# An adaLN transformer block on one core: output sent in two parts with an accumulating transfer, a new setup, a shorter calibration, explicit table loads, and the last pair split

## What is computed

```python
mod = (silu(c) @ wmod).reshape(B, 6, 1, -1)                 # B = 16 sequences, D = 256
sa, ca, ga, sb, cb, gb = mod[:, 0], ..., mod[:, 5]          # ga, gb: magnitude at least 0.25
h = layernorm(x) * (1 + ca) + sa                            # x: (16, 512, 256), float32
x = x + ga * attn(h)                                        # causal softmax of |q.k|/16, then Wo
h = layernorm(x) * (1 + cb) + sb
x = x + gb * ffn(h)
# ffn: cluster score -> calibrate (sigmoid, 8 knots, piecewise linear) -> argmax over 8 clusters
#      tile score of the chosen cluster -> calibrate -> argmax over 8 tiles -> gather 1 of 64 tiles
#      comp = tanh(gelu(h W1 + b1) W2 + b2); mag = relu(comp . w1 + b1') . w2' + b2'
#      y = layernorm(h + mag * direction * scale) * gamma + beta
```

## Time and profile before

| | us |
|---|---|
| three runs of the kernel | 470.21, 470.64 (median), 472.34 |
| the profiled execution | 471.67 |
| its span, first to last instruction | 469.8 |
| its mean granted TensorE clock | 0.931 of 2.4 GHz |

### The profile page before, as it was taken

The page is one execution under the profiler, slowest core; times in us unless marked ns, Lnnn a source line. Parts: engine busy times, 40 slices in busy tenths (PEclk is TensorE's granted clock), DMA queues, the critical chain, the costliest instruction groups (busy, mean ns, idle before and its releaser), DMA issues.

```text
span 469.8 us, 7656 instructions
## 1 busy us (share of the span) xinstructions
PE 399.8 (85%) x2072; PEld 308.7 (66%) x2072; DVE 398.5 (85%) x1367; ACT 296.5 (63%) x645; POOL 67.4 (14%) x82
## 2 busy tenths in 40 slices
PE   2697899999999999899989998999899999463330
PEld 2555578777777877687768776877677778452220
DVE  4417637387859899999999999999999899999996
ACT  2230365877698769676967697769776976651400
POOL 1002310302020002400250015001400220031040
PEclk9977899999999999999999999999999999796565
DMA  8503102101200213112310231122100210040112
GB/s 292 142 30 105 74 23 79 35 1 45 69 23 1 69 45 114 45 28 86 114 45 25 91 112 47 22 91 86 50 1 1 73 64 1 4 130 0 35 57 89
DMA packets 26234, 28.72 MB, mean 61 GB/s; under 512 B 3888, under 2 KB 21552, under 8 KB 26192
## 3 DMA queue, kind: packets, MB, share of 16 engines
q1 hardware_dynamic: 24160, 26.38, 17.8%
q10 hardware_dynamic: 2032, 1.85, 1.2%
HBM read 19.77 MB, written 8.45 MB: 60 GB/s over the span
## 4 chain that ended last, share of the span: by engine, by line
DVE 45%; PE 42%; issue 8%; ACTq 2%; ACT 2%; DVEq 0%
PE bank L511 8%; PE bank L530 8%; PE bank L490 6%; PE bank L500 6%; PE bank L553 3%; DVE y L1278 3%; DVE y L1246 3%; DVE x L1091 3%; DVE res L1288 3%; DVE st L1254 2%; DVE probs L1077 2%; DVE st L1046 2%; PE bank L520 2%; ACTq L680 2%; DVE v L1070 2%
## 5 line engine op out<-in xcount | busy, mean ns | idle before, releaser
L511 PE MATMUL bank<-h,g 128*128 128x128 f32 (+3 forms) x256 | 80.2, 444 | 4.9 <-DVE v L1070 4.9
L978 POOL TENSOR_TENSOR res<-x,gb_row 128x512 f32<-128x512 f32 x32 | 44.5, 1407 | 268.3 <-DMA out<-res 268.3
L530 PE MATMUL bank<-v,probsT 128*128 128x257 f32 x320 | 79.1, 382 | 0.0
L500 PE MATMUL bank<-m_ga,h 128*128 128x258 f32 x256 | 68.8, 394 | 5.2 <-DVE rows L1360 3.2
L530 PEld LDWEIGHTS bank<-v,probsT 128*128 128x128 f32 x320 | 57.1, 190 | 6.6 <-DVE y L1246 0.3
L490 PE MATMUL bank<-h,a_sb 128*128 128x512 f32 x128 | 60.4, 595 | 0.0
L511 PEld LDWEIGHTS bank<-h,g 128*128 128x128 f32 x256 | 44.7, 195 | 22.1 <-issue 8.5
L500 PEld LDWEIGHTS bank<-m_ga,h 128*128 128x128 f32 x256 | 47.7, 197 | 15.7 <-issue 4.3
L736 ACT ACTIVATE bank<-bank,v 128x128 f32<-128x128 f32 (+1 forms) x64 | 31.7, 495 | 41.4 <-PE bank L511 29.1
L1077 DVE CUSTOM_DVE_ANT_0 probs<-bank,cmask 128x128 f32<-128x128 f32 (+1 forms) x64 | 31.1, 485 | 23.3 <-ACT bank L736 23.3
L742 ACT ACTIVATE probs<-probs,negmax 128x128 f32<-128x128 f32 (+1 forms) x64 | 35.5, 557 | 5.9 <-DVE negmax L1077 5.9
(11 more groups left out here) (167 smaller groups left out, 770.1 us busy)
## 6 DMA issues: line engine op xcount, KB each, us to landing
x<-in_L_attn_x SPq DMA_DIRECT2D x16, 512.0 KB, 3.5
out<-res SPq DMA_DIRECT2D x16, 512.0 KB, 3.0
a_row<-gate_rows SPq DMA_DIRECT2D x16, 256.0 KB, 3.2
gb_row<-gate_rows SPq DMA_DIRECT2D x16, 256.0 KB, 3.2
wide<-in_L_wmod ACTq DMA_DIRECT2D x2, 768.0 KB, 7.6
res<-in_L_attn_Wq SPq DMA_DIRECT2D x1, 256.0 KB, 5.0
res<-in_L_attn_Wk SPq DMA_DIRECT2D x1, 256.0 KB, 7.3
res<-in_L_attn_Wo SPq DMA_DIRECT2D x1, 256.0 KB, 10.1
```

What stands on the lines that cost most here:

```text
L500: last = mm(ps[:, 0:VW], h[s][:, c, t * P:(t + 1) * P], m_ga[p % 2][s][:, c, :], start=(c == 0), stop=(c == KC - 1))
L511: last = mm(ps[:, 0:w], g[s][:, c, t * P:(t + 1) * P], h[s][:, c, 0:w], start=(c == 0), stop=(c == KC - 1))
L530: last = mm(ps[:, 0:D + 1], probsT[s][t][:, j * P:(j + 1) * P], v_sb[s][:, j, 0:D + 1], start=(j == 0), stop=(j == t))
L978: gp.tensor_tensor(res[:, 2 * u:2 * u + 2, :], x2[p % 2][s][:, t, :], gb_row[p % 2][s][:, 1:2, :].broadcast_to([P, 2, D]), ALU.add).then_i ...
```

## The change

Seven edits go together.

1. **The output is sent in two parts.** x2 is sent to `out` by SP as soon as it is there (`xo`). `ob` adds the gated beta row instead of `res`, so `res` holds the gated FFN alone, and POOL issues a transfer of it that adds into `out` (`ay`). `base` remains for the last two groups only, which are sent whole.
2. **calibrate** has ten instructions in place of twelve: the line of each of the seven segments is evaluated, masked and summed.
3. **Tables.** After `gelu` and after `tanh` the set that holds ln and exp is loaded by name.
4. **The last pair is two groups** of four tiles (groups 7 and 8) in the FFN; groups 0 to 6 are pairs.
5. **Setup.** silu is taken on the turned c; the gate row of sequences 0 and 1 is made directly on 128 partitions (`su_gax`, `sd_gax`), without the way through memory; biases are loaded by POOL; copies move from DVE to ACT; two of the first `a_xh` and one `a_h` are done by DVE; the signature and table constants are made by POOL (`sp_sig`, `sp_rest`) after the first `ms`.
6. **Orders**: every engine has a written order for the first steps, a loop for k = 5 to 7, and a written order for the end.
7. **The bank table** is new.

```diff
+            def xo(g, i):
+                p, s = of_group(g, i)
+                spq.wait_ge(x2_rdy, NT * (before(g) + i + 1))
+                spq.dma_start(out_v[GROUPS[g][i]], x2[p % 2][s][:, :, :]).then_inc(x2_sent[p % 2][s], 16)
...
+            def ay(g, i):
+                pool.wait_ge(alone_rdy, NT * (before(g) + i + 1))
+                pool.wait_ge(x2_sent[g % 2][i], 16 * (g // 2 + 1))
+                gp.dma_start(out_v[GROUPS[g][i]], res[:, NT * i:NT * (i + 1), :], accum_op=ALU.add).then_inc(summed[i], 16)
...
             def ob(g, t):
+                if g < BY_SUM:
+                    if t % NT == 0:
+                        need(dve, summed[t // NT], 16 * g)
+                    rest = gb_row[g % 2][t // NT][:, 1, :]
+                else:
+                    dve.wait_ge(base_rdy, 2 * (before(g) - before(BY_SUM)) + t // 2 + 1)
+                    rest = res[:, t, :]
-                stt(out=res[:, t, :], in0=y[:, t, :], scalar=ln3["rstd"][:, t:t + 1], in1=res[:, t, :],
-                    op0=ALU.mult, op1=ALU.add).then_inc(res_rdy, 1)
+                stt(out=res[:, t, :], in0=y[:, t, :], scalar=ln3["rstd"][:, t:t + 1], in1=rest,
+                    op0=ALU.mult, op1=ALU.add).then_inc(alone_rdy, 1)
...
             def base(g, u):
+                pool.wait_ge(summed[0], 16 * BY_SUM)
+                need(pool, sent, 16 * (g - BY_SUM))
...
+                if i == 3:
+                    m(ts(low, pos, 0.5, ROUND - 0.5, ALU.max, ALU.add))
+                elif i == 4:
+                    m(stt(out=back, in0=low, scalar=-ROUND, in1=pos, op0=ALU.add, op1=ALU.subtract))
+                elif i == 5:
+                    m(tt(own, by_segment(low), by_score(steps[:, 0:K1]), ALU.is_equal))
+                elif i == 6:
+                    m(tt(line, by_segment(back), by_score(knot_lin[:, 1, :]), ALU.mult))
+                elif i == 7:
+                    m(tt(line, line, by_score(knot_lin[:, 0, :]), ALU.add))
+                elif i == 8:
+                    m(tt(line, line, own, ALU.mult))
+                else:
+                    m(red(val[:, 0:n_], line, X, ALU.add))
...
+        GROUPS = [(2 * p, 2 * p + 1) for p in range(PAIRS - 1)] + [(B - 2,), (B - 1,)]
+        BY_SUM = PAIRS - 1
```

More of the change, by code:

```diff
@@ new lines, in _ @@
+                for i in range(1, 3):
+                    b_pt(k - 1, 0, i)
+                b_exp(k - 1, 0, 3)
+                b_abs(k - 1, 1, 0)
+            a_xh(7, 0, 0)
+            c_ga(4, 2)
+            a_xh(7, 0, 1)
+            b_exp(6, 1, 0)
+            for i in range(3, 6):
+                c_ga(4, i)
+            a_xh(7, 0, 2)
+            b_abs(6, 1, 1)
+            c_ga(4, 6)
+            tanh(4)
+            b_pt(6, 0, 3)
+            c_ga(4, 7)
+            gelu(5)
+            exp_table()
@@ new lines, in _ @@
+            c_h2(6, 3)
+            c_oht(5, 0)
+            b_exp(7, 0, 1)
+            c_fs(6, 0)
+            y_gs(4)
+            for i in range(1, 3):
+                c_fs(6, i)
+            ecl(6)
+            for i in range(0, 3):
+                c_ga(5, i)
+            b_exp(7, 0, 2)
+            c_oht(5, 1)
+            c_ga(5, 3)
+            b_exp(7, 0, 3)
+            c_ga(5, 4)
+            b_g(7, 1, 1)
+            b_pt(7, 0, 1)
+            c_ga(5, 5)
+            b_pt(7, 0, 2)
@@ new lines, in _ @@
+            c_ga(5, 6)
+            b_abs(7, 1, 0)
+            c_ga(5, 7)
+            b_exp(7, 1, 0)
+            b_pt(7, 0, 3)
+            for i in range(1, 3):
+                b_abs(7, 1, i)
+            elo(6)
+            b_pt(7, 1, 0)
+            for i in range(1, 3):
+                b_exp(7, 1, i)
+            c_gs(7)
+            gelu(6)
+            exp_table()
+            for i in range(0, 2):
+                c_xh(7, i)
+            b_pt(7, 1, 1)
+            for i in range(2, 4):
+                c_xh(7, i)
@@ new lines, in _ @@
+            b_abs(7, 1, 3)
+            c_h2(7, 0)
+            b_pt(7, 1, 2)
+            c_h2(7, 1)
+            b_exp(7, 1, 3)
+            y_gs(5)
+            for i in range(0, 2):
+                c_fs(7, i)
+            ecl(7)
+            c_oht(6, 0)
+            for i in range(0, 2):
+                c_ga(6, i)
+            b_pt(7, 1, 3)
+            tanh(6)
+            c_ga(6, 2)
+            gelu(7)
+            exp_table()
+            c_oht(6, 1)
+            for i in range(3, 8):
+                c_ga(6, i)
@@ L933, in _ @@
+            y_gs(7)
+            c_oht(8, 0)
+            for i in range(0, 4):
+                c_ga(8, i)
+            y_gs(8)
         @block.gpsimd
@@ L1114, in _ @@
[L1114 to L1124 removed]
+                    dve.wait_ge(st2_rdy, NT * before(g + 1))
@@ new lines, in _ @@
+            clc(0, 9)
+            b_ri(1, 0, 2)
+            b_st(1, 0, 1)
+            b_x2(1, 0, 2)
+            clb(0, 0)
+            b_st(1, 0, 2)
+            b_ri(1, 0, 3)
+            b_x2(1, 0, 3)
+            clb(0, 1)
+            b_ri(1, 1, 0)
+            b_x2(1, 1, 0)
+            for i in range(2, 5):
+                clb(0, i)
+            pick(0, 0)
+            b_st(1, 0, 3)
+            c_b2(0)
+            pick(0, 1)
+            b_ri(1, 1, 1)
+            b_st(1, 1, 0)
+            loc(0, 0)
@@ new lines, in _ @@
+            b_ttr(7, 1, 3)
+            loc(6, 9)
+            lob(6, 0)
+            y_var(5, 0)
+            lob(6, 1)
+            y_var(5, 1)
+            for i in range(2, 4):
+                lob(6, i)
+            for i in range(2, 4):
+                y_var(5, i)
+            b_st(7, 1, 0)
+            lob(6, 4)
+            b_ri(7, 1, 1)
+            oh(6, 0)
+            b_x2(7, 1, 1)
+            oh(6, 1)
+            clc(7, 0)
+            for i in range(0, 3):
+                oa(5, i)
```

2887 lines of the change are left out of this document (2092 added, 795 removed), and 16 rows, old and new, of the table BANK.

## The result

The changed kernel takes 479.25 us (median of 4 runs, 478.46 to 482.28) where the kernel before takes 471.49 beside it (median of 4). The ratio is 1.016, with a 95% interval of 1.008 to 1.024: slower, against a forecast of 454.0 and outside its range of 443 to 467. The profiled execution took 478.56 us, its span is 476.8, against 469.8 before.

A forecast was written before the change was run, and what follows sets the result against it. The prediction took DVE to bound the loop at 47.5 us a superstep, PE close behind at 45.8. Its terms, -10 - 5 + 4 - 6 = -17 against the span of 469.8, gave 452.8, stated as 454.0 us, range 443 to 467.

The forecast's parts named there:

- Part 1: DVE in the loop: shorter calibrate and four fewer base cut DVE's need from 47.3 to about 43.3 us; -5 us.
- Part 2: Output transfers: accumulating ones land in about 6 us, hidden in the loop; POOL's issues cost DVE at most 2.1 us a superstep.
- Part 3: Table loads on ACT: 18 more, 23 us, costed at nothing in the loop; 4 + 2 us of waits at the end.
- Rival (c): ACT in the loop: table loads lie in the open ahead of what PE waits for; 471 to 480 us, chance 0.07.
- Part 4: Setup and first pair: V_ of the first sequence starts at about 30 in place of 40.75; sum -10 us.
- Part 5: The end, last pair divided: +4 us on the last x2 tile, then -6 us on DVE after it.
- rival (d): Accumulating transfer gives the gain back: over 40 us ob waits each superstep, at 20 only the end pays, 466; chance 0.07.
- (a): Rival: the loop stays at 47.5 us as another wait replaces the one removed; total 462, chance 0.22.

The follow-up runs named there:

- e4: The kernel before with the new calibrate, base cut to one column for the first seven pairs and ob reading the gate's row: 461.05 us, ratio 0.982.
- e11: The kernel before with new calibrate, x2 sent by SP, 14 accumulating transfers, base for the last pair only; orders, setup, tables and end of before: 461.45 us, ratio 0.977.
- e3: The changed kernel with its 14 accumulating transfers replaced by plain ones of the same size sent by SP: 481.81 us, ratio 1.026.
- e12: The changed kernel with its 14 transfers still issued by POOL at the same places, but as plain writes: 481.88 us, ratio 1.020.
- e5: The changed kernel with Gelu and Tanh computed as Identity and named loads left out but the first, one table load left of 35: 459.09 us.
- e1: The changed kernel with 12 of 35 table loads removed, one Gelu set serving Tanh and Gelu in groups 1 to 4, 6 and 7: 463.51 us, ratio 0.987.
- e10: e1 with two table loads put back into each looped superstep, in the stretch where ACT idles: 462.83 us against 463.51 for e1.

## Why the prediction was wrong, point by point

**The bound** was read rightly. DVE at 47.5 and PE at 45.8 behind it: e4 and e11 run at 45.8 once DVE is relieved, and PE's 1.7 us a superstep was all there was to gain in the loop.

**Part 1** said -5 us for the loop. Alone it gave -5.3 (188.4 to 183.1). In the changed kernel without loads it was -3.1, in another order of the loop. The mechanism was right. What the sum had nothing for is what it gives outside the loop, 5.7 us of the span in e4.

**Part 2.** The landing was taken at 6 us and is 6.5. That it hides in the loop holds (e3, e12). What was mis-sized is what sending from POOL costs DVE: bounded by 0 and 1.07 each from the earlier trace rows, at most 2.1 a superstep, and measured 2.8 (1.7 and 2.1 on two instructions, less what the products cost at their places in e3). So "DVE busy about 43.5" came out as 46.0. The bound was put on the issue, but an issue alone stretched nothing (e11). The issue brought `ms` to a place where DVE runs instructions that wait for it, and made it 0.5 us longer. It changed nothing in the total, since another engine was later. The Trainium skill (SBUF — State Buffer, Who interferes with whom) was cited for POOL's transfer waiting for its descriptors while DVE holds the port. No row here shows such waiting: the landing was 6.3 to 6.5 us, with DVE 95% busy and nothing to compare it with. What the rows show is the other direction, a DVE instruction that waited for POOL's product.

**Part 3 is the step that failed.** It costed the loads "at nothing in the loop, where ACT idles 11 us", and put 6 us at the end. They cost 23.7 us of the span, by e5: 1.5 up to `FS(1)`, 6.2 in the four supersteps where the sum had 0, 9.0 from there to the last x2 tile where it had 0 too, and 7.0 after it where it had 4.5. The 11 us were right as a sum (9.5 after the change), but I took them as cover without asking where they lie. All of the idle time stands in the second half of the superstep, and the four loads stand in the first, in 22 us of ACT work without a gap, ahead of `gath`, `probsT` and `h` that PE waits for. The prediction said that "the cover is gone where a load stands ahead of what PE waits for next"; the new order of ACT was there to be read, and ACT's windows inside a superstep of before too. Rival (c) named mechanism and place, its price was 471 to 480 and the time is 479.25; its chance of 0.07 was too low. That the time meets its upper price is in part luck: that price counts 32 us of loads and all other terms as forecast, where the loads cost 20 to 24 and the other terms came out 5 to 10 us dearer. What spoke for more was also in the text: old order Gelu and then Tanh with nothing between, new order Tanh, load, Gelu, load.

The 12 loads of e1 cost 1.31 us each by the medians (15.7 / 12), 1.39 by the spans and 1.1 by the ratios. This is an average of 0.7 to 2.2 (1.04 in the middle supersteps, 2.2 where the clock fell), so its closeness to the load's own 1.283 is chance. The Trainium skill (ScalarE: Activation LUTs, What ACT_TABLE_LOAD costs) gives 2.66 us with a drain; the prediction went by the earlier trace rows instead, and the runs bear the row out: with the two loads of e10 one behind the other the second starts 1.28 us after the first (293.10, 294.38). The same page (Table sets: the hidden batching unit) says to group calls by set and not by function. That rule speaks against this change, e1 agrees with it, and I had not weighed it.

**Part 4** said -10 us. `V_` of the first sequence starts at 24.98 (30 was said), `FS(1)` comes 12.0 us earlier (9 to 12 with the starts of the other executions). Right in kind and size, though `V_` gained 15.8 us and not 10.7, and the 8 us that PE was said to lose in 40.7 to 77 are 6.5 by the row: 2.0 of waits and 4.5 of clock.

**Part 5** said +4 us up to the last x2 tile and -6 after it. Up to the tile it is +6.4 without loads (85.3 against 78.9) and +15.4 with them; after it -6.5 without loads, -4.8 in e1, and +0.5 with all loads. (For the end without ACT's waits the text says -9, but its own terms give -13.7 + 3.2 = -10.5.) The signs were right without the loads, and the loads were missing again: they are 9.0 of the 11.4 us missed ahead of the tile, where I had looked for them only behind it.

**The sum** without ACT's waits would have been about 449.5; e5 has 459.1 (its profiled run 454.9). Of the 25 us by which the forecast missed, the loads are 16 to 19 (20.2 by the medians or 23.7 by the spans, less the 4.5 counted net). The other 5 to 10 lie in the new orders of the loop and the end: by the profiled run 2 are part 1's in the loop, 2 the last x2 tile's and 4 the time after it, less 3.5 that the start gained over its forecast in that run. Which moves cost them no run shows. In rival (d) the price together with (a) is 466 + 8 = 474, not 470; it was not met.

## What to carry to other kernels

Idle time of an engine covers added work only where it lies. Before costing an instruction at nothing on an engine with 20% idle time, cut the superstep into pieces and look whether the gap stands beside the place of the new instruction, or behind it. Where two functions share a table set, let nothing of another set come between them, and where a load by name is needed, put it into a gap: the same load cost 0, 0.2 or 1.0 us of a full superstep by its place alone, and 2.2 where PE's wait behind it was followed by a lower clock. And when several edits come in one change, try them apart: parts 1 and 2 alone in the old order were 2.3% faster than before, the whole was 1.6% slower.

## What the runs showed of the hardware that I had not expected

Small DVE instructions were held up until a product of POOL beside them ended: 0.18 to 1.92 and 0.62 to 2.75 us with an accumulating issue ahead of the product, 0.20 to 1.27 in the kernel before with none. They ended 0.03 to 0.49 us behind the product in all these rows. An issue that stood alone held up none.

Two DVE instructions began before the product's row does (224.00 against 224.08, 244.76 against 245.24); why they too waited for its end, the traces don't say.

Behind an accumulating issue the same product took 1.78 us, behind a plain one 1.28, by itself in e3 1.27 to 1.29.

Where PE had waited 2.47 us behind two table loads, its granted clock was 0.57 from 334 to 338 us; where it had waited 0.93 at the same place (e1), it stayed at 1.00.

The accumulating transfer of 512 KB takes 1.3 us of POOL to issue and lands in 6.5 us, the plain one from POOL 0.79 and 4.5, the plain one from SP 3.0 to 4.9 (medians: `res` in before 3.0, in e3 3.2, in e4 4.4, x2 in the changed kernel 4.8 and in e3 4.9).

A set can be loaded by name for a function that is not the one it is called after: with `gelu_and_others` loaded in e1, Tanh and then Gelu ran without a further load.
